# A context stage that reads x already transposed, folds layer norm into the values and sends deviations through memory

## The reference, cut to what matters

```
xn = (x - mean(x)) / sqrt(var(x) + 1e-5)            # per token, over 256
v  = xn @ Wv.T + bv                                 # 64 tokens x 128, per batch
t  = ctx @ Wt.T + bt                                # 256 rows x 128, per batch
x  = x + (v @ t.T) / max(|v| * |t|, 1e-8)           # 64 x 256, per batch
```

## Time and profile before

| | us |
|---|---|
| median of 3 runs (521.0 to 521.76) | 521.6 |
| profiled execution, its own time | 522.03 |
| its span | 520.1 |
| context stage: PE's first context matmul to `attention_step(0)` | 7.50 to 114.03 |
| PE busy, of the span | 500.8 (96%) |
| ACT busy | 347.7 (67%) |
| DVE busy | 346.5 (67%) |
| POOL busy | 241.2 (46%) |

### The profile page before, as it was taken

One profiled execution on the slowest core, in us unless ns is written; L12 is line 12 of the kernel. 1 busy time (PEld: TensorE's weight loads), 2 busy tenths in 40 slices (PEclk: granted clock), 3 DMA queues, 4 the chain that ended last, 5 costly groups with the idle time before them and its releaser, 6 DMA issues.

```text
span 520.1 us, 14430 instructions
## 1 busy us (share of the span) xinstructions
PE 500.8 (96%) x4324; PEld 396.9 (76%) x4325; DVE 346.5 (67%) x1054; ACT 347.7 (67%) x837; POOL 241.2 (46%) x405
## 2 busy tenths in 40 slices
PE   7999999998999999999999999999999999999993
PEld 5555555566888888788878888778989999999992
DVE  3578766636899999898998989997563332323231
ACT  2776777668888998889888888887453334343430
POOL 2356655436334445564655556552753233232322
PEclk9999999999999999999999999999999999999997
DMA  8964446200001233323322322237656666656620
GB/s 311 330 199 160 157 162 197 81 0 22 22 23 27 83 109 113 88 86 107 113 88 84 77 81 68 66 121 240 193 202 230 208 221 201 225 185 209 194 83 9
DMA packets 35617, 69.88 MB, mean 134 GB/s; under 512 B 5664, under 2 KB 23714, under 8 KB 35568
## 3 DMA queue, kind: packets, MB, share of 16 engines
q1 hardware_dynamic: 31680, 60.19, 37.4%
q0 software_dynamic: 3456, 8.85, 4.6%
q10 hardware_dynamic: 432, 0.26, 0.2%
HBM read 54.21 MB, written 11.60 MB: 127 GB/s over the span
## 4 chain that ended last, share of the span: by engine, by line
PE 84%; DVE 6%; issue 4%; DMA 1%; POOL 1%; ACT 1%; SPq 0%; DVEq 0%; POOLq 0%; ACTq 0%
PE psum L1383 12%; PE psum L1396 12%; PE psum L1325 8%; PE psum L1276 6%; PE psum L1163 6%; PE psum L1284 5%; PE psum L1297 5%; PE psum L1244 4%; PE psum L1337 4%; PE psum L1206 3%; PE psum L1213 3%; PE psum L1175 3%; PE psum L1189 3%; PE psum L1178 3%; PE psum L1217 3%
## 5 line engine op out<-in xcount | busy, mean ns | idle before, releaser
L1383 PEld LDWEIGHTS psum<-arena,ring 128*128 128x128 f32 x640 | 77.3, 192 | 3.5 <-issue 1.7
L1383 PE MATMUL psum<-arena,ring 128*128 128x128 f32 x640 | 78.2, 275 | 0.9 <-ACT arena L1107 0.6
L1396 PE MATMUL psum<-w_s,arena 128*128 x320 | 76.0, 381 | 0.0
L927 DVE TENSOR_TENSOR arena<-psum,tok 128x256 f32<-128x256 f32 x40 | 17.0, 424 | 84.6 <-PE psum L1396 83.1
L1101 ACT ACTIVATE arena<-psum 128x256 f32<-128x256 f32 x40 | 15.4, 385 | 86.6 <-PE psum L1163 58.7
L1396 PEld LDWEIGHTS psum<-w_s,arena 128*128 128x128 f32 x320 | 57.8, 190 | 6.5
L490 POOL TENSOR_TENSOR ov<-o_n,v_s 128x256 f32<-128x256 f32 x32 | 23.5, 735 | 80.3 <-DVE o_n L694 80.3
L1071 ACT ACTIVATE arena<-kT,head_mask 128x256 f32<-128x256 f32 x128 | 57.3, 499 | 0.0
L545 POOL DMA_INDIRECT out<-arena,token_of x40 | 39.9, 999 | 19.7 <-POOL token_of L537 14.1
L1107 ACT ACTIVATE arena<-psum,b_s 128x128 f32<-128x128 f32 x160 | 45.6, 375 | 3.5 <-PE psum L1383 2.2
L795 DVE TENSOR_REDUCE smax<-psum 128x16 f32<-128x1024 f32 x32 | 39.0, 1218 | 1.6 <-PE psum L1297 0.4
(11 more groups left out here) (193 smaller groups left out, 1123.3 us busy)
## 6 DMA issues: line engine op xcount, KB each, us to landing
ring<-w SPq DMA_DIRECT2D x40, 512.0 KB, 3.6
w_s<-ctxT SPq DMA_DIRECT2D x15, 768.0 KB, 5.0
w_s<-w SPq DMA_DIRECT2D x16, 448.0 KB, 3.5
slot_rec<-routed SPq DMA_DIRECT2D x40, 132.0 KB, 3.0
tok<-x SPq DMA_DIRECT2D x16, 256.0 KB, 5.8
v_swap<-v_s SPq DMA_DIRECT2D x64, 64.0 KB
routed<-pad_rec SPq DMA_DIRECT2D x1, 1980.0 KB, 10.8
tok<-b SPq DMA_DIRECT2D x14, 128.0 KB, 3.2
```

The costliest lines, as they stand in the source:

```text
L1383: mm = pe.matmul(hid_bank(p)[:, f * P:(f + 1) * P], w1_s[:, r, c * F + f * P:c * F + (f + 1) * P], xgT[:, p, c * P:(c + 1) * P], start=c = ...
L1396: mm = pe.matmul(bank(2 + q, D), hidT[:, q, f * P:(f + 1) * P], w2_s[:, bass.ds(e * (FC * D) + f * D, D)], start=f == 0, stop=f == FC - 1)
```

## The change

- The input `xT` holds x transposed on the host's side of the layout. From pair 4 (`TURNED = 4`) on, SP loads it in front of the context of the same pair, and PE multiplies it straight by weights `wvc_s` whose column means are taken out (made once, in the opening, from two matmuls and one DVE instruction). Pairs 0 to 3 go the old way.
- The values are then not divided by the deviation. What is kept is v times the deviation: DVE adds bias times deviation (`std_b`, the deviation of each token in every partition) when it takes the product out of PSUM, and the factor 1/deviation comes in with the square sum of v (`pair_rvar`) and with `cos` (`pair_rstd`), which is now written by two instructions of 256 elements.
- `std_b` is made by way of memory: POOL computes the deviations of pair n in `deviation(n)`, which stands in POOL's step n-4 behind `tok_sum`; ACT issues the store of 128x2 numbers in its step n-2 after waiting for `a_std`, and in its step n-1, after waiting for `std_out`, the load that spreads them over all partitions (128 KB).
- ACT loses L1005 (`vT`) and L1009 from pair 4 on and squares `vT` from SBUF; the square sum of v on PE moves from the end of step t to the middle of step t+1.

The core of the diff:

```diff
@@ block.sync, load_tokens
                     need(sp, s["t_psum"], i - 3)
+                    if not isinstance(i, int) or i >= TURNED:
+                        sp.dma_start(xT_s[:, k], xT[bass.ds(i, 1)].rearrange("o p j -> (o p) j")).then_inc(ctx_in[k], 16)
                     sp.dma_start(ctx_in_sb[:, k], ctxT[bass.ds(i, 1)].rearrange("o p j -> (o p) j"))\
                         .then_inc(ctx_in[k], 16)
@@ block.gpsimd, context_step(j, k)
+                def deviation(n, p):
+                    pair = bass.ds(n * 2, 2)
+                    need(pool, s["a_stats"], n + 1)
+                    need(pool, s["a_rstd"], n - 1)
+                    need(pool, s["a_std"], n - TURNED - 1)
+                    pool.tensor_scalar(pair_vareps[:, p], pair_mv[:, p, :, 1], LN_EPS, 1.0 / LOG_SCALE, ALU.add, ALU.mult)\
+                        .then_inc(s["a_vareps"], 1)
+                    need(pool, s["a_vareps"], n + 1)
+                    pool.tensor_tensor(pair_rstd[:, pair], pair_vareps[:, p], mhalf[:, :].broadcast_to([P, 2]), ALU.pow)\
+                        .then_inc(s["a_rstd"], 1)
+                    need(pool, s["a_rstd"], n + 1)
+                    pool.tensor_tensor(pair_rvar[:, pair], pair_rstd[:, pair], pair_rstd[:, pair], ALU.mult)
+                    pool.tensor_tensor(pair_std[:, pair], pair_vareps[:, p], pair_rstd[:, pair], ALU.mult)\
+                        .then_inc(s["a_std"], 1)
...
                     pool.tensor_tensor(both, both, cos[:, q, :], ALU.add).then_inc(s["tok_sum"], 1)
+                if paired(n) and not (isinstance(j, int) and j < 0):
+                    deviation(n, p)
@@ block.vector, context_step(j, k), with v = j + 1
+                if paired(v) and not (isinstance(v, int) and v < TURNED):
+                    need(dve, s["v_psum"], v + 1)
+                    need(dve, s["dots_psum"], v - 1)
+                    need(dve, std_in[p], arrivals(v - TURNED, p, 2, 16))
...
+                    dve.scalar_tensor_tensor(vT[:, p, :].rearrange("f (h t) -> f h t", h=2),
+                                             std_b[:, p, :].rearrange("f (t h) -> f h t", h=2), xbs_s[:, :],
+                                             bank(p, 2 * P).rearrange("f (h t) -> f h t", h=2), ALU.mult, ALU.add)\
+                        .then_inc(s["v_sbuf"], 1)
...
+                if paired(j + TURNED) and not opening:
+                    raw_statistics(j + TURNED, k, q)
+                    statistics(j + TURNED, q)
...
                 if paired(j):
                     need(dve, s["norms_inv"], j + 1)
                     need(dve, s["tok_sum"], j - 1)
-                    dve.scalar_tensor_tensor(cos[:, q, :], rnorm[:, q, :], LOG_SCALE ** 0.5, bank(3), ALU.mult, ALU.mult)\
-                        .then_inc(s["cos_sbuf"], 1)
+                    for h in range(2):
+                        c = slice(h * SC, (h + 1) * SC)
+                        made = dve.scalar_tensor_tensor(cos[:, q, c], rnorm[:, q, c], pair_rstd[:, bass.ds(j * 2 + h, 1)],
+                                                        bank(3)[:, c], ALU.mult, ALU.mult)
+                    made.then_inc(s["cos_sbuf"], 1)
@@ block.scalar, context_step(i, k), with t, n, w = i, i + 1, i - 2
                 if paired(w):
                     need(act, s["norms_kept"], w + 1)
                     need(act, s["cos_sbuf"], w - 1)
+                    act.activation(rnorm[:, p, :], norm[:, p, :], ACT.Ln).then_inc(s["norms_log"], 1)
                     need(act, s["norms_log"], w + 1)
                     act.activation(rnorm[:, p, :], rnorm[:, p, :], ACT.Exp, scale=-0.5).then_inc(s["norms_inv"], 1)
+                if paired(n) and not turned(n):
+                    need(act, s["std_out"], arrivals(n - TURNED, 0, 1, 16))
+                    need(act, s["v_sbuf"], n - 1)
+                    act.dma_start(std_b[:, q, :],
+                                  deviations[bass.ds(n, 1)].rearrange("o p h -> o (p h)").broadcast_to([P, 2 * P]))\
+                        .then_inc(std_in[q], 16)
+                if paired(i + 2) and not turned(i + 2):
+                    need(act, s["a_std"], i + 2 - TURNED + 1)
+                    act.dma_start(deviations[bass.ds(i + 2, 1)].rearrange("o p h -> (o p) h"),
+                                  pair_std[:, bass.ds(i * 2 + 4, 2)]).then_inc(s["std_out"], 16)
                 if paired(t):
+                    need(act, s["vnorm_psum"], t - 1)
+                    if isinstance(t, int) and t < TURNED:
...
+                        act.activation(vT[:, p, :], bank(1, 2 * P), ACT.Identity, bias=xbv_s).then_inc(s["v_sbuf"], 1)
+                        act.activation(vsq[:, p, :], bank(1, 2 * P), ACT.Square, bias=xbv_s).then_inc(s["vsq_ok"], 1)
+                    else:
+                        need(act, s["v_sbuf"], t + 1)
+                        act.activation(vsq[:, p, :], vT[:, p, :], ACT.Square).then_inc(s["vsq_ok"], 1)
@@ block.tensor, context_step(i, k)
                     for c in range(KC):
+                        if raw:
+                            mm = pe.matmul(bank(p, 2 * P), wvc_s[:, c, :], xT_s[:, k, c * 2 * P:(c + 1) * 2 * P],
+                                           start=c == 0, stop=c == KC - 1)
...
-                if paired(n):
+                if isinstance(n, int) and 0 <= n < TURNED:
...
+                if paired(u) and not (isinstance(u, int) and u < TURNED):
+                    norm_of_v(u, q, q)
```

More of the change, by code:

```diff
@@ L277, in build @@
         ctx_in = [sem(f"ctx_in{n}") for n in range(4)]
+        std_in = [sem(f"std_in{n}") for n in range(2)]
         swap_in = [sem(f"swap_in{n}") for n in range(2)]
@@ L604, in context_step @@
                     need(dve, s["a_stats_raw"], n + 1)
-                if paired(t) and not opening:
-                    normalise()
[L607 to L611, removed]
+                    for h in range(2):
+                        whole = dve.bn_aggr(pair_mv[:, p, h, :], pair_stats[:, p, h])
@@ new lines, in statistics @@
+                    whole.then_inc(s["a_stats"], 1)
+                opening = isinstance(j, int) and j < 0
+                if opening:
+                    if paired(t):
+                        normalise()
+                    raw_statistics(j + TURNED, k, q)
+                    statistics(j + TURNED, q)
+                if isinstance(j, int) and j == 0:
+                    normalise()
+                if isinstance(j, int) and j == -3:
+                    dve.wait_ge(s["csum_psum"], 1)
+                    dve.scalar_tensor_tensor(wvc_s[:, :, :], bank(2, H).unsqueeze(1).broadcast_to([P, KC, H]), -1.0 / D,
+                                             wv_s[:, :, :], ALU.mult, ALU.add).then_inc(s["centre_ok"], 1)
@@ new lines, in norm_of_v @@
+                def norm_of_v(j, q, column):
+                    need(dve, s["vnorm_psum"], j + 1)
+                    need(dve, s["norms_kept"], j - 1)
+                    dve.tensor_tensor(vnorm[:, q, :], bank(column)[:, 2 * P:2 * P + 2], pair_rvar[:, bass.ds(j * 2, 2)],
+                                      ALU.mult).then_inc(s["vnorm_sbuf"], 1)
+                if paired(j) and not (isinstance(j, int) and j < TURNED):
+                    need(dve, s["a_std"], j - TURNED + 1)
+                    norm_of_v(j, q, q)
@@ L616, in context_step @@
                     raw.then_inc(s["stats_raw"], 1)
+                    need(dve, s["stats_raw"], b + 1)
+                    need(dve, s["std_ok"], b - 1)
+                    for h in range(2):
+                        whole = dve.bn_aggr(mv[:, p, h, :], stats[:, h, :])
+                    whole.then_inc(s["stats_ok"], 1)
                 if paired(j):
@@ L1157, in _ @@
             pe.wait_ge(s["first_made"], 5)
-            for n in range(12):
+            for n in range(11):
                 pe.matmul(bank(7, P), ident[:, :], ones[:, :], start=True, stop=True)
+            pe.wait_ge(s["wv_in"], 16)
+            for c in range(KC):
+                mm = pe.matmul(bank(2, H), ones[:, :], wv_s[:, c, :], start=c == 0, stop=c == KC - 1)
+            mm.then_inc(s["csum_psum"], 1)
             def turn(tile, source, signal):
@@ L1167, in context_step, with norm_of_v @@
                 t, p, n, u, q = i, k % 2, i + 1, i - 1, (k - 1) % 2
+                def norm_of_v(v, r, column):
+                    need(pe, s["vsq_ok"], v + 1)
+                    for j in range(2):
+                        mm = pe.matmul(bank(column)[:, 2 * P + j:2 * P + j + 1], vsq[:, r, j * P:(j + 1) * P], ones[:, 0:1],
+                                       start=True, stop=True)
+                    mm.then_inc(s["vnorm_psum"], 1)
                 if paired(t):
@@ new lines, in context_step @@
+                if paired(t) and isinstance(t, int) and t < TURNED:
+                    norm_of_v(t, p, 1)
+                if isinstance(t, int) and t == NB - 3:
+                    pe.wait_ge(s["consts_in"], 16 * RESTS)
+                    pe.wait_ge(s["v_sbuf"], t + 1)
```

(12 more changed lines are left out.)

124 lines of the change are left out of this document (63 added, 61 removed).

## The result

| | before | after |
|---|---|---|
| median, us | 521.68 (4 runs, 521.0 to 521.86) | 538.8 (4 runs, 537.44 to 539.4) |
| ratio | | 1.0321, interval 1.0298 to 1.0344 |
| profiled execution, its own time / span | 522.03 / 520.1 | 537.44 / 535.6 |
| PE's first attention matmul (`attention_step(0)`) starts at | 114.03 | 128.84 |

The kernel is 3.2% slower, 17.1 us; 535.1 was forecast. The profiled execution is the fastest of the four, 15.4 us above the one before. Its context stage ends 14.8 us late; the rest of the span is 406.8 us, 406.1 before.

A forecast was written before the change was run, and what follows sets the result against it. PE was taken as the limit now (96% busy); a new ring of 7.78 us per step would start PE's step 15 13.06 us late, plus 0.47, in all 13.5: 535.1 us against the median, range 529 to 543.

The forecast's parts named there:

- The ring: Context stage: ACT's wait for `a_std` closes a chain through DVE and POOL, 7.78 us per step against PE's 6.06.
- Its length: Serial links from ACT's L996 to the next L996 in the context stage, summed to 7.78 us per step.
- The start: L996 of ACT's step 2 stays at 20.54, nothing ahead of it changes; PE's step 15 starts at 120.72.
- the moved square sum: The last pair's square sum of v on PE moves behind the attention stage's start: 0.47 us more.
- `cos` in two halves: DVE writes `cos` by two instructions of 256: 0.88 us taken, bounds 0.69 and 0.96.
- DVE's new instruction: DVE gains one 256-element instruction out of PSUM per pair, about 0.44 us.
- the two new issues: ACT gains two DMA issues per pair, 0.45 us each.
- What leaves PE: PE's transposes of pairs 4 to 15 go: 12 x 0.53 = 6.4 us, a new PE step of 6.06 us.
- the faster rival: The ring at ACT's wait for `a_std` doesn't close, PE's 6.06 us step rules: 515.2 against the median; 8%.
- The way through memory: Store and load of the deviations are hidden by the ring; a store landing costs nothing up to 7.3 us.
- this rival: Slower by DMA latency: a store landing later than 7.3 us delays the load's issue and all behind it, 541; 5%.
- The clock: Rival: PE's idle time of 1.7 us per step lowers its granted clock, up to 52 us more, 587; 3%.

The follow-up runs named there:

- Experiment 4: The changed kernel with one more POOL power instruction inside `deviation`, ahead of `a_std`: 547.84 us, ratio 1.0509 to the kernel before.
- the third chip: The changed kernel repeated unaltered on another chip, beside the kernel before: 542.27 us, ratio 1.0408 to the kernel before.

## Why the prediction was right

- **The ring** was the cause, and its links were those predicted. Experiment 4 lengthens it by 0.68 us per step, 8.4 in all, and the kernel by 9.0.
- **Its length** was mis-sized, 7.78 against 8.06. ACT's store is issued 0.28 us after POOL's product ends, in place of my 0.03: with a dynamic index the sequencer runs register instructions behind the wait (83 + 35 + 29 ns in the last fence of the first section, 0.15 of the 0.28). In the last two steps, where the index is a constant, the ring turns in 7.82. `tok_sum` to `deviation` took 1.35 instead of 1.21. The other links fell within 0.1. Over steps 4 to 13 that is 80.2 us instead of 77.8.
- **The start** was 1.06 us earlier (L1066 at 19.48 instead of 20.54), since the first rows of x landed sooner and the second statistics started at 7.12 instead of 8.19. That is mostly when loads landed; other traces have 19.4 to 21.0 there. PE's step 15 started at 122.54, forecast 120.72. The rest of the span behind the context stage took 0.7 us more than before, where I had 0.5 for the moved square sum.
- **`cos` in two halves** took 0.87, forecast 0.88; DVE's new instruction 0.48, forecast 0.44; the two new issues 0.36 each, not 0.45.
- **What leaves PE** is worth what was forecast once the rings are open: 514.8 and 515.1 measured, 515.2 in the faster rival.
- **The way through memory** is the step that was too kind. The row of 3.9 us was a load into SBUF at the start; the store took 6.3 us in the middle and 7.4 at most, just at the 7.3 that I had called free. So the load was issued not 1.32 us into ACT's step, the earliest by my sum, but when the store had landed, up to 4.64 us into it (L1075 at 89.53, L1066 at 84.89), and that just fitted. The Trainium skill's warning (DMA: Bandwidth & Descriptors, the anatomy of one DMA) that a last write towards memory can be surprisingly long fits; its 2 us does not, and the page fits that figure to DMAs issued through GpSimd, not to those of ACT's hardware queue. On the third chip three stores took 8.2, 8.5 and 8.2 us, and their steps 8.48, 9.13 and 8.70: 2.3 us of the 4.6 by which that span is longer (540.2 against 535.6), with 0.4 from a later start and 1.7 from behind the context stage. That late stores also explain why the median lies 1.4 above the profiled execution is likely but not shown, since only one execution was profiled. The 5% for this rival were too few: it acted beside the forecast, not instead of it.
- **The clock** fell in some stretches of PE's idle time, as its rival said, and cost the ring nothing. It took up part of that idle time: PE's waits ahead of L1324 sum to 12.2 us over ten steps, where I had 1.7 us in each.

## What to carry to other kernels

A wait in an engine's queue holds all that stands behind it. Ask of every new wait whether what it waits for depends, through other engines, on something that this engine issued just before it or will issue just behind it; then add up the turn, and do it again for the ring behind the first. A round trip through memory is free only with a lead longer than its slowest landing, and with the store in front of the older load's wait.

## What the runs showed of the hardware

- A store of 128 pieces of 8 bytes to memory took 2.9 to 9.8 us to land beside bulk loads, with medians of 6.0 to 7.0 in the twelve traces. Loads of 1 KB into SBUF took 3.9 in the opening of the kernel before and 4.7 to 5.2 in the middle of the changed kernel's stage.
- A DMA issue of ACT started 0.28 us after its wait was met where its address came from a register, and 0.04 us after where it was a constant (POOL's product ends at 113.85 there, the issue starts at 113.89).
- The granted clock of PE fell in some stretches of the changed kernel and not in others with as much idle time. Two of them (length, busy time of each engine, clock, DMA share, GB/s):

```profile
60.00:70.00 10.00, 8.05 (x31) 4.19 (x32) 4.21 (x14) 5.48 (x8) 4.24 (x15) 0.83 0.62 189
70.00:80.00 10.00, 7.75 (x36) 3.66 (x34) 5.33 (x18) 3.62 (x6) 4.53 (x10) 1.00 0.74 157
```

With 1.16 us of matmuls in each idle stretch it stayed at 1.00 through the context stage on the third chip. The swing itself is what the Trainium skill says of repeated short gaps (TensorE: Matmul & The Clock Gate, the second HAM failure mode); here it was hidden.
